# K and Q restacked in whole rows, the prologue written as schedule words, a new order of the fill, and 64 transposes of the identity on TensorE

## The reference

```python
x = x + tanh(g_xattn) * attention(layernorm(x), ctx, ctx)   # 16 heads of depth 16
x = x + tanh(g_ffn) * ffn(layernorm(x))
# attention: qh = q@wq+bq, kh = k@wk+bk, vh = v@wv+bv; softmax(qh.kh / 4) @ vh; @ wo + bo
# ffn: (gelu(x@w1+b1) @ w2 + b2) * (sum of the two largest router probabilities, renormalised)
#      w1 is 256x1024, w2 is 1024x256, the router has 8 experts
```

## Time and profile before

| | us |
|---|---|
| median of 3 runs (732.95 to 735.4) | 734.27 |
| the profiled execution, its own time | 734.14 |
| its span, first to last instruction | 732.1 |
| TensorE busy with matmuls (PE) | 696.4 |
| VectorE busy (DVE) | 514.4 |
| ScalarE busy (ACT) | 402.5 |
| GpSimd busy (POOL) | 321.3 |

### The profile page before, as it was taken

The page is one execution under the profiler, slowest core; times in us unless marked ns, Lnnn a source line. Parts: engine busy times, 40 slices in busy tenths (PEclk is TensorE's granted clock), DMA queues, the critical chain, the costliest instruction groups (busy, mean ns, idle before and its releaser), DMA issues.

```text
span 732.1 us, 20618 instructions
## 1 busy us (share of the span) xinstructions
PE 696.4 (95%) x7648; PEld 652.3 (89%) x7648; DVE 514.4 (70%) x1298; ACT 402.5 (55%) x800; POOL 321.3 (44%) x476
## 2 busy tenths in 40 slices
PE   3688999999999999999999999999999999999987
PEld 2566888999999999999999999999999999988966
DVE  6378788777776777776777777777677777766422
ACT  2124666465564646556564746556474655656753
POOL 4313436444434545434344544343454543424246
PEclk9979999999999999999999999999999999999999
DMA  4868789866748585764658486684758576450000
GB/s 146 179 198 169 187 189 224 155 170 137 178 104 174 125 187 132 171 167 124 158 111 206 103 187 154 129 190 110 165 122 182 139 171 150 104 93 3 15 1 27
DMA packets 84021, 103.21 MB, mean 141 GB/s; under 512 B 9589, under 2 KB 79570, under 8 KB 83922
## 3 DMA queue, kind: packets, MB, share of 16 engines
q1 hardware_dynamic: 83282, 101.12, 59.9%
q10 hardware_dynamic: 640, 0.77, 0.5%
HBM read 65.05 MB, written 34.05 MB: 135 GB/s over the span
## 4 chain that ended last, share of the span: by engine, by line
PE 87%; DVE 4%; ACT 2%; issue 2%; POOL 2%; SPq 1%; DMA 1%; ACTq 0%; POOLq 0%; DVEq 0%
PE P L921 42%; PE S L951 13%; PE T L963 11%; PE OT L978 11%; PE P L1004 4%; PE TR L987 2%; PE TR L1060 1%; DVE NEGM L764 1%; PE TR L1043 1%; ACT PROBS L678 1%; PE TR L994 1%; PE TR L936 1%; DVE XN L832 1%; PE TR L1028 1%; DMA QS<-q_parts 1%
## 5 line engine op out<-in xcount | busy, mean ns | idle before, releaser
L764 DVE TENSOR_REDUCE NEGM<-S 112x1 f32<-112x375 f32 x512 | 267.3, 539 | 73.4 <-PE S L951 71.3
L678 ACT ACTIVATE PROBS<-T 125x448 f32<-125x448 f32 x384 | 196.2, 543 | 106.0 <-PE T L963 98.4
L951 PE MATMUL S<-KS,QS 96*112 96x376 f32 x512 | 181.7, 361 | 9.6 <-DVE NEGM L764 6.3
L963 PE MATMUL T<-QS,KS 98*125 98x224 f32 x768 | 150.6, 282 | 3.1 <-ACT PROBS L678 1.7
L963 PEld LDWEIGHTS T<-QS,KS 98*125 98x125 f32 x768 | 129.3, 188 | 10.0 <-ACT PROBS L678 4.6
L582 POOL CAST HT_HI<-HG 128x224 fp32r<-128x224 f32 x128 | 47.3, 369 | 152.0 <-ACT HG L701 144.0
L951 PEld LDWEIGHTS S<-KS,QS 96*112 96x112 f32 x512 | 91.3, 180 | 23.5 <-DVE NEGM L764 13.0
L566 POOL CAST CT_HI<-CTRAW 128x750 fp32r<-128x750 f32 x31 | 25.1, 810 | 161.7 <-DMA CTRAW<-in_ctxT 151.0
L584 POOL TENSOR_TENSOR HT_LO<-HG,HT_HI 128x224 fp32r<-128x224 f32 x128 | 85.2, 666 | 10.3
L978 PE MATMUL OT<-PROBS,VA 125*17 125x112 f32 x3072 | 87.6, 260 | 0.0
L701 ACT ACTIVATE HG<-P,B 128x224 f32<-128x224 f32 x128 | 57.2, 447 | 53.4 <-PE P L921 52.2
(11 more groups left out here) (113 smaller groups left out, 1496.8 us busy)
## 6 DMA issues: line engine op xcount, KB each, us to landing
KS<-k_parts SPq DMA_DIRECT2D x90, 375.0 KB, 7.1
CTRAW<-in_ctxT SPq DMA_DIRECT2D x32, 375.0 KB, 3.5
k_parts<-KHI SPq DMA_DIRECT2D x30, 375.0 KB, 3.9
k_parts<-KLO SPq DMA_DIRECT2D x30, 375.0 KB, 4.5
QS<-q_parts SPq DMA_DIRECT2D x96, 112.0 KB, 4.9
X<-in_x SPq DMA_DIRECT2D x16, 224.0 KB, 3.6
q_parts<-QHI SPq DMA_DIRECT2D x32, 112.0 KB, 2.4
q_parts<-QLO SPq DMA_DIRECT2D x32, 112.0 KB, 2.3
```

The costliest lines, as they stand in the source:

```text
L678: act.activation(PT[0:KN, k, pp * 4 * SQ:(pp + 1) * 4 * SQ], T_BANK[i % 2][0:KN, 0:4 * SQ], ACT.Exp, scale=SCALE).then_inc(exp_done, 1)
L764: dve.tensor_reduce(NEGM[:, b.par, i:i + 1], S_BANK[i % 2][0:SQ, 0:SK], AX.X, ALU.max, negate=True).then_inc(max_done, 1)
L951: pe.matmul(S_BANK[i % 2][0:SQ, 0:SKP], QS[0:96, i, b.ring * SQ:(b.ring + 1) * SQ], KS[0:96, b.ring, i // 2, :], start=True, stop=True).th ...
L963: mm = pe.matmul(T_BANK[i % 2][0:KN, r * 2 * SQ:(r + 1) * 2 * SQ], KS[0:98, prv.ring, pair, k * KN:(k + 1) * KN], QS[0:98, 2 * pair:2 * pa ...
```

## The change

1. **Restack in whole rows.** `k_parts` becomes 32 rows of 8 x 376 elements, so that a row of KS is one piece of 12,032 bytes instead of 8 pieces of 1,500; `q_parts` likewise, with rows of 7,168 bytes instead of 8 pieces of 896. The order of rows in KS becomes low, high, high; the two high thirds are loaded by one DMA whose source repeats with a leading step of 0. Stores now have a destination whose outermost dimension is 4. K has 376 columns instead of 375. Heads change their order in KS, QS, NEGM, VA and WO accordingly. QS is split by group, so that each group's half is zeroed apart.
2. **Prologue as words.** The loads (`ld.0` to `ld.7`) and memsets (`zp`, `zh`, `zi`, `zr`, `zq`, `zo`, `zy`, `zv`) stand in the lists, and each has its own semaphore. WK and CT are loaded first. W1 is loaded and split in four parts like W2 (`lw`, `w`), and the low parts of WV, W1 and W2 move from VectorE to GpSimd.
3. **New order of steps -2 to 5.** `ORDER` and steps 32 to 34 are as before.
4. **`hot.0` to `hot.7`**: 8 transposes each of the 128x128 identity into T bank 1. Nothing reads them.

```diff
-        QS = sb("QS", [128, NH, RING * SQ], F32R)
+        QS = sb("QS", [128, 2, 2, NPAIR, TOK], F32R)
-        KD = nc.dram_tensor("k_parts", (2, 2, NPAIR, 32, SK), F32, kind="Internal").ap()
-        QD = nc.dram_tensor("q_parts", (2, 2, DC, 4, DH, TOK), F32, kind="Internal").ap()
+        KD = nc.dram_tensor("k_parts", (2, 2, 32, NPAIR * SKP), F32, kind="Internal").ap()
+        QD = nc.dram_tensor("q_parts", (2, 2, DH, NPAIR * TOK), F32, kind="Internal").ap()
...
-                        sp.dma_start(QS[r0:r0 + DH, hh:NH:2, cols].bitcast(F32),
-                                     QD[part, hh].rearrange("c p r n -> r (c p) n")).then_inc(qs_loaded, 16)
+                        sp.dma_start(QS[r0:r0 + DH, g.gpar, hh, :, :].bitcast(F32),
+                                     QD[part, hh].rearrange("r (g n) -> r g n", g=NPAIR)).then_inc(qs_loaded, 16)
...
-                        sp.dma_start(KD[nn.par, 0].rearrange("(c p) r n -> (p r) c n", c=DC),
+                        sp.dma_start(KD[nn.par, 0].rearrange("r (p n) -> p r n", p=4),
                                      KHI[:, :, :].bitcast(F32)).then_inc(khi_stored, 16)
...
-                        for row in (0, 2):
-                            sp.dma_start(KS[32 * row:32 * row + 32, nn.ring, :, 0:SK].bitcast(F32),
-                                         KD[nn.par, 0].rearrange("g r n -> r g n")).then_inc(ks_loaded[nn.par], 16)
+                        sp.dma_start(KS[32:96, nn.ring, :, :].rearrange("p g n -> p (g n)").bitcast(F32),
+                                     KD[nn.par, 0].unsqueeze(0).to_broadcast([2, 32, NPAIR * SKP])
+                                     ).then_inc(ks_loaded[nn.par], 16)
...
-                            sp.dma_start(QD[0, hh].rearrange("c p r n -> (p r) c n"),
+                            sp.dma_start(QD[0, hh].rearrange("r (p n) -> p r n", p=4),
                                          QHI[64 * hh:64 * hh + 64, :, :].bitcast(F32)).then_inc(qhi_stored, 16)
...
+                    if op in SPLIT and op not in LOW_ON_DVE:
+                        raw_in, parts, loaded, split = SPLIT[op]
+                        pool.wait_ge(split, 1)
+                        pool.tensor_tensor(parts[1][:, :, :], raw_in, parts[0][:, :, :].bitcast(F32),
+                                           ALU.subtract).then_inc(split, 1)
...
-            pe.wait_ge(dve_zeroed, 3)
-            pe.wait_ge(ident_done, 2)
...
+                    if op == "hot":
+                        if i == 0:
+                            pe.wait_ge(ident_done, 2)
+                        for n in range(8):
+                            pe.transpose(T_BANK[1][:, 0:128], IDENT[:, :], IDENT[:, :])
...
-    (-2, """cl+1 xl-2 l1 xn cx ct wk k.0 wv k.1 wq xt ka.2 l1-2 kd.1 q.0 q.1 qs v.0 cl v.1 xn-2 tg v.2 v.0-1
-       v.1-1 kd.0 ct-1"""),
+    (-2, """hot.0 zp zh ld.3 hot.1 ld.2 zi zr wk cx hot.2 l1 tg wq k.0 k.1 w.0 hot.3 xn ka.1 ct xt ld.0 ld.4 l1-2
+       hot.4 xn-2 ka.2 q.0 q.1 zq wv xt-2 ld.6 hot.5 ld.1 zo zy w.1 lw.0 hot.6 v.0 ld.7 cl+1 v.1 v.2 q.0-2
+       q.1-2 v.0-1 ct-1 ld.5"""),
```

More of the change, by code:

```diff
@@ L49 @@
 HR = 3
-W2_PART = 2
+W_PART = 512
 DIRECT = 2
@@ L418, in load @@
                 sp.dma_start(dst, src).then_inc(loaded, 16)
[L420 to L429, removed]
-            load(X[:, 1, :, :], x[GB:2 * GB].rearrange("j q d -> q j d"), x_loaded[1])
             def at(first, n):
@@ L626, in step @@
                         act.activation(parts[0][:, :, :], raw_in, ACT.Copy).then_inc(split, 1)
-                    if op == "w2":
-                        part = w2_part(i)
-                        act.wait_ge(w2_loaded, 16 * (i + 1))
-                        act.activation(W2[0][:, part, :], W2_IN[:, 0:part.stop - part.start, :],
-                                       ACT.Copy).then_inc(w2_split, 1)
+                    if op == "w":
+                        _, raw_in, high, _ = w_part(i)
+                        act.wait_ge(w_loaded, 16 * (i + 1))
+                        act.activation(high, raw_in, ACT.Copy).then_inc(w_split, 1)
                     if op == "ka":
-                        act.wait_ge(klo_done if i == 1 else khi_done, nn.count(2, 2))
+                        act.wait_ge(klo_done if i == 0 else khi_done, nn.count(2, 2))
                         move_k(act, nn, i)
@@ L730, in step @@
                     bank = P_BANK[BANKS.get((now.k, stage), 0)]
-                    if op in SPLIT:
+                    if op == "zp":
+                        for part in CT:
+                            dve.memset(part[:, :, :, SK:SKP].bitcast(F32), 0.0).then_inc(pads_zeroed, 1)
+                    if op == "zq":
+                        dve.memset(QS[:, 0, 1, :, :].bitcast(F32), 0.0).then_inc(qs_high_zeroed, 1)
+                    if op == "zo":
+                        dve.memset(OT[:, :], 0.0).then_inc(ot_zeroed, 1)
+                    if op in SPLIT and op in LOW_ON_DVE:
                         raw_in, parts, _, split = SPLIT[op]
@@ L1047, in step @@
                         take(p, gelu_done, pg.group(FC, i + 1))
-                        if pg.k == 0 and i == 0:
-                            pe.wait_ge(w1_split, 2)
+                        if pg.k == 0 and i in (0, FC // 2):
+                            pe.wait_ge(w_split, 4 if i == 0 else 8)
                         pe.wait_ge(x2tlo_done, pg.group(1, 1))
```

241 lines of the change are left out of this document (144 added, 97 removed).

## The result

The changed kernel takes 1062.28 us (median of 4 runs, 1057.28 to 1071.27), the kernel before, run beside it, 734.36. The ratio is 1.448, interval 1.436 to 1.460. The prediction said 723. What came is the first rival, to which it gave 0.18, and for which it had worked out 895.

The account below looks back on a forecast made before the run. TensorE was taken to bound the steady part, so only the fill could gain: -3.0 - 1.5 - 2.5 - 1.5 - 3.5 + 1.0 = -11.0, from 734.1 to 723 us. The range was 711 to 735.

Parts of the forecast that it names:

- the first rival: K's high load on 2 engines, stores on 4, so TensorE waits in each pair: about 895 us, chance 0.18.
- A rule against this change: Restack DMAs: engines may have to divide the outermost dimension; new leading sizes 2 and 4 would then confine load and stores.
- Whole rows, 0 in the steady part: Steady part: whole-row transfers give 0, as TensorE has no idle time there that a transfer could end.
- With only the load confined just hidden.: Pair of batches: with only K's high load on two engines, their occupancy is 41.5 of 41.8 us, just hidden.
- Loads first, -3.0 and -1.5: Fill: WK and CT loaded first, first K matmul at about 7.4, -3.0 us; chain to first score, about 30, -1.5.
- VectorE relieved, -2.5: Fill: low parts of W1, W2 and WV leave VectorE, shortening waits for its reductions, -2.5 us.
- GpSimd's work at nothing: Fill: GpSimd's nine added low parts, some 10 us, are hidden in its idle time and cost nothing.
- Whole rows, -1.5: Fill: longer DMA rows cut the restack's landing from 7.1 to about 4 us, giving -1.5 us.
- The clock, -3.5: Fill: transposes raise TensorE's clock earlier; a third of at most -10.7 us taken, -3.5.
- the transposes, +1.0: Fill: the 64 identity transposes themselves cost TensorE time, mostly hidden in waits, +1.0 us.
- that rival: Fill: the transposes don't raise the clock, early V, Q and K run low: 728 us, chance 0.20.

Follow-up runs that it names:

- e9_rows_q16: Changed kernel with K's high load as two, K's stores as four of 32 rows, Q's parts stored with row blocks outermost, all on 16 engines: 738.6 us.
- fourth kernel: Changed kernel with K's and Q's parts stored with row blocks outermost and K's high load as two, no DMA confined: 733.5 us, ratio 0.9985.
- e5: The fourth kernel without the 64 transposes of the identity: 732.0 us, ratio 0.9976.
- e12: The seventh kernel without the 64 transposes of the identity: 727.0 us, ratio 0.990.
- seventh kernel: The fourth kernel with WQ's load ahead of BV's, ScalarE's wait for BV and gates later, and GpSimd's memset of KS's ones behind the seventh score: 725.8 us.

## Why the prediction was wrong

- **The count of engines.** The failing step is the weighing under "A rule against this change": the trace of before bore the count out for one DMA, BV's, and I held it for less likely that it holds for a leading size of 2 or 4. It does (shares of 0.13 and 0.25). The row itself was read a little too simply: BV's wasn't the last large load in the queue, X's was issued behind it at 5.44, so its share of 0.39 isn't BV's alone. The change adds exactly such sizes, so this one point decided everything, and 0.18 was too little for a rule that the one row at hand agreed with. "Whole rows, 0 in the steady part" fell with it.
- **The rival's size, 895 us.** Its term, a wait of 14.3 us in each of 12 pairs, measured 15.1. That they agree is luck: the 14.3 came from an occupancy sum, and the same sum put the loss at nothing where the load alone is confined and 190.6 us were measured. A pair took 61.6 us, not the 56 of the sum. Three things were left out: the lower clock that the waits bring (58.0 us), the fill, where the same waits cost 93.2 us, and the drain, 2.0.
- **"With only the load confined just hidden."** Refuted by 929.2 us. Occupancy is the wrong measure: what counted here is how late everything lands that stands behind a confined transfer, and whether the next confined transfer waits for it. K's stores, at 25 of 41.8 us, cost 72.6 (67.5 against e9_rows_q16); Q's, 31.9.
- **Loads first, -3.0 and -1.5.** The first K matmul was right (6.72 in the fourth kernel, 6.76 in the changed one, 7.4 foretold, 10.39 before). The first score stands at 34.59 in the fourth kernel instead of 30: the chain was held at WQ, whose load stood behind BV's and the gates'. I had counted what is ahead of CT and not what is ahead of WQ. With both mended it is 32.74.
- **VectorE relieved, -2.5, GpSimd's work at nothing.** The low parts are hidden, but a 2.6 us memset beside XN was not: 2.5 us of VectorE, and TensorE's wait behind it fell from 3.71 to 1.24 us without it. I had named CT's low part as the cover to watch; it was the wrong instruction.
- **Whole rows, -1.5.** The restack lands in 6.6 to 6.8 us, not about 4, in the kernels without confinement (7.1 before), the DMA share of the 12 pairs is 0.60, not about 0.4 (0.65 before), and whole rows are no faster than pieces. The 13.6 GB/s for each engine that I laid to short pieces have another cause, which stays open.
- **The clock, -3.5, the transposes, +1.0.** They raise the clock, so that rival's mechanism is refuted; but no gain can be told in e5 and e12. TensorE then waits 5.8 us in the fourth kernel and the clock falls back, and it falls twice more: after its first rise it is low for 27.2 us, where I had foretold less than 20 in all.

The sum over the whole fill, -11.0, is approached only in the best version (725.8 against 734.7 us of the kernel before beside it, -8.8), after two further edits that the prediction didn't have, and with two of its six terms (whole rows, the clock) at nothing.

## What to carry to other kernels

Before a DMA's shape is changed, write down the outermost dimension of both its sides: here a size of 2 or 4 there put it on two or four engines, whatever the bytes, and a loss of 45% can come from two lines that only seem to merge transfers. Store in a layout in which the partition blocks are outermost and let the load do the regrouping in its inner dimensions. The mark in a profile is a low DMA share under a chain of DMA waits, with landings of unconfined transfers that have tripled (3.5 to 10.2 us). And where an early gain doesn't reach the end of a fill, look for the one transfer, or the one memset on the neighbouring engine, that the next link waits for.

## What the runs showed of the hardware

- Transposes raise TensorE's clock too: behind 24 of the identity alone, a K matmul took 0.33 us instead of 0.52. How soon varies: in the seventh kernel's profiled execution the first three K matmuls behind them still took 0.65, 0.52 and 0.44 us. (The Trainium skill, "TensorE: Matmul & The Clock Gate", section "Part 4: PE-mode transpose", says they don't count in the same way; here the measurement decides.)
- The two confined engines move 26.5 GB/s each; sixteen together move 205 to 238 GB/s with K's parts, 13 to 15 each, with pieces of 1,500, 3,008 or 12,032 bytes, though W1's load had 25.6 each on sixteen. What holds K's loads back stays open.
- Issuing a DMA isn't always short: with the load and the stores confined, the issue of X's load held SyncE for 10.40 us, against 0.36 before.
